# Conv attention on Trainium2: values as two float16 halves, a mix on four 32-column groups, sums from the exponential, and key copies on GpSimd

## The chip, the cores and the metric

The kernel runs on one core of one Trainium2 chip. The metric is the device time of one execution, in microseconds (us); the number quoted is the median of the runs. The engines are TensorE (PE; its weight loads are PEld), VectorE (DVE), ScalarE (ACT) and GpSimd (POOL); SyncE (SP) issues DMAs here.

## The reference

Two decoder layers run over x of 4 x 1024 x 256. The diff touches one of their six stages, the second layer's self attention, in which each head's scores pass a convolution of width 3 over the keys that mixes the 16 heads:

```python
Q = (query @ Wq.T + bq).reshape(b, s, h, dh).transpose(0, 2, 1, 3)      # h = 16, dh = 16
K, V = ...                                                             # likewise
scores = jnp.einsum('bhqd,bhkd->bhqk', Q, K) / np.sqrt(dh).astype(np.float32)
x = scores.transpose(0, 2, 1, 3).reshape(b * s, h, s)
x = lax.conv_general_dilated(x, conv_w, window_strides=(1,), padding=[(1, 1)], ...)
x = x + conv_b[None, :, None]
weights = jax.nn.softmax(x.reshape(b, s, h, s).transpose(0, 2, 1, 3), axis=-1)
out = jnp.einsum('bhqk,bhkd->bqhd', weights, V).reshape(b, s, e)
return out @ Wo.T + bo
```

## The kernel before

The stages run one behind the other. The conv attention (`stage_conv_attention`, L1858) moves the convolution to the keys: for each output head the three shifted keys of all heads are scaled with that head's taps and added, which gives one key matrix of 256 x 1024. So scores have a contraction of 256 instead of 16, and each is computed from high and low parts of queries and keys (QH, QL, KH, KL), three products for each of two blocks of 128 channels.

**Units.** A unit is 128 query rows of one head against 1024 keys. Eight units are a head, four are a group, 16 heads are a batch, 4 batches make 512 units. Every engine has its own hand-written loop over the units (`for u in range(ALL + TAIL)`), and semaphores tie the loops together. What is done for one unit `u`:

- TensorE, `scores(u)` (L2061): twelve matmuls of 512 columns into one of three PSUM buffers of 1024 columns. It waits until the low half of unit u - 3 is made, and at a head's first unit until both low key parts are there (`key_low`).
- VectorE, `maximum(u)` (L2320, L2324): negative maximum over the keys, then the bias for the exponential. After it `low_probs(u - 1)` (L2329).
- ScalarE, `exps(u)` (L2210): exponential in place in PSUM; `high_probs(u)` (L2217): its high half as float16 into `halves`. VectorE's `low_probs(u)` is the low half. Both are turned by a transposing DMA that SyncE issues (L1994) into `probsT`, one of three buffers of two units each.

**Groups.** Once in four units, after the scores of units 3 and 7 of a head, TensorE runs the mix (`mix_values`, L2075) of the four units that were turned last: for each of two pairs of units, 8 key tiles and 2 halves, so 32 matmuls of 256 columns. The stationary operand is `V`: 64 columns, of which 48 hold the values in three bfloat16 parts of 16, one holds ones (its product is the sum of the probabilities) and the rest zeros. The two halves write to PSUM partitions 0 to 63 and 64 to 127. ScalarE moves the result to SBUF (`move_mixT`, L2226), TensorE turns it back after units 1 and 5 (`turn_back`, L2085), and VectorE normalizes after units 2 and 6: L2339 adds the two sums, L2341 the six parts, L2345 inverts, L2348 multiplies.

**Keys of the next head.** While head hh is scored, GpSimd and ScalarE make the keys of hh + 1. For each of the two channel blocks GpSimd scales the middle tap (L2012) and adds the other two (L2016, L2020), which ScalarE has scaled (`tap`, L2200). ScalarE makes these in units 0 (block 0, third tap), 1 (block 1, first tap), 3 (block 1, third tap) and 6 (block 0 of the head after, first tap), each between the exponential and the high half. ScalarE then copies the high parts (`high`, L2206, in units 2 and 5), and GpSimd subtracts them for the low ones (L2027), both after all its additions.

**Values** are split by ScalarE (L2262) and VectorE (L2375, L2380) in turn, in four steps for each half of the heads, in units 101 to 104 of a batch for the next one and 5 to 8 for its second half.

**Extra work.** Between the units the next batch is prepared: normalization at units 36 to 48 of a batch, queries at 52 to 64, keys at 68 to 80, values at 84 to 96, one step in each group, after the scores of units 0 and 4 of a head; the last batch's output is turned and projected at units 3 to 16. All share one PSUM bank with `turn_back`.

## Time and profile before

| | us |
|---|---|
| median of 3 runs | 4005.49 (4002.89 to 4012.54) |
| span of the profiled execution | 4015.4 |
| conv attention in it: first score matmul to last turning of a mix | 867.0 to 2738.2 |
| score matmuls of 512 columns | 6144 in three groups, 681.7 + 637.7 + 637.3 busy |
| mix matmuls of 256 columns | 4096, 249.1 busy |

The profile is of one execution, so its span is set beside the median and not taken for it. Busy time of TensorE counts matmuls that overlap, and its ends are modelled; where a sentence needs TensorE's pace, the starts of its weight loads are read.

### The profile page before, as it was taken

The numbers are of one execution on the slowest core, as the hardware profiler recorded it, in microseconds if no ns is written. First come the engines' busy times: TensorE is split into PE (matmuls) and PEld (weight loads), VectorE is DVE, ScalarE is ACT, GpSimd is POOL, SyncE is SP. The second block draws the span as 40 slices with busy tenths as digits, with TensorE's granted clock in tenths as the row PEclk, the third lists the DMA queues.
The fourth block names the chain that finished last, engine by engine and source line by source line (L and its number), as shares of the span: only waits on it lengthen the run. The fifth ranks groups of instructions, "written<-read, shape, count | busy, mean of one in ns | idle before, by whom it ended". The sixth has DMA issues, their size and how long they took to land. (4 is left out here: it accounts for less than half of the span.)

```text
span 4015.4 us, 64275 instructions
## 1 busy us (share of the span) xinstructions
PE 3489.2 (87%) x22159; PEld 2787.0 (69%) x22159; DVE 2936.8 (73%) x5979; ACT 2563.5 (64%) x3388; POOL 1828.4 (46%) x1128
## 2 busy tenths in 40 slices
PE   6867623379999999999999999996889898799999
PEld 4645421257777777877777788884667667689999
DVE  4568789878878888788878888884767666464347
ACT  2334445558778887788878888882667666344433
POOL 0034410026655565565655656651767676360005
PEclk9988956599999999999999999997999999799999
DMA  1047700058878887787878878882559477643224
GB/s 49 0 95 128 147 5 1 1 142 150 143 139 148 140 147 140 139 153 136 151 137 141 153 140 155 153 157 56 99 91 171 84 124 137 199 138 97 76 78 144
DMA packets 1571361, 470.22 MB, mean 117 GB/s; under 512 B 1507175, under 2 KB 1565160, under 8 KB 1569768
## 3 DMA queue, kind: packets, MB, share of 16 engines
q1 hardware_dynamic: 1564903, 449.40, 58.8%
q0 software_dynamic: 6144, 16.79, 1.3%
q8 instruction: 179, 2.93, 0.3%
q14 instruction: 135, 1.10, 0.1%
HBM read 49.00 MB, written 39.58 MB: 22 GB/s over the span
## 5 line engine op out<-in xcount | busy, mean ns | idle before, releaser
L2320 DVE TENSOR_REDUCE d_neg_max<-psum 128x1 f32<-128x1024 f32 x512 | 624.9, 1220 | 247.9 <-PE psum L2061 242.3
L2210 ACT ACTIVATE psum<-psum,d_bias 128x1024 f32<-128x1024 f32 x512 | 557.6, 1089 | 335.3 <-DVE d_bias L2324 331.8
L2061 PE MATMUL psum<-d_KH,d_QH 128*128 128x512 f32 x2048 | 681.7, 414 | 17.7 <-DVE d_halves L2329 13.2
L2329 DVE SCALAR_TENSOR_TENSOR d_halves<-psum,d_halves 128x1024 f16<-128x1024 f32 x512 | 622.9, 1217 | 24.0 <-ACT d_halves L2217 21.2
L2061 PE MATMUL psum<-d_KL,d_QH 128*128 128x512 f32 x2048 | 637.7, 393 | 0.0
L2061 PE MATMUL psum<-d_KH,d_QL 128*128 128x512 f32 x2048 | 637.3, 392 | 0.0
L2020 POOL TENSOR_TENSOR d_KC<-d_KC,d_tap_of 128x1024 f32<-128x1024 f32 x126 | 301.8, 2395 | 559.9 <-ACT d_tap_of L2200 559.9
L2217 ACT ACTIVATE d_halves<-psum 128x1024 f16<-128x1024 f32 x512 | 521.7, 1019 | 3.5
L2061 PEld LDWEIGHTS psum<-d_KH,d_QH 128*128 128x128 f32 x2048 | 360.5, 189 | 129.4 <-issue 43.4
L2061 PEld LDWEIGHTS psum<-d_KH,d_QL 128*128 128x128 f32 x2048 | 385.1, 188 | 86.6
L2061 PEld LDWEIGHTS psum<-d_KL,d_QH 128*128 128x128 f32 x2048 | 384.8, 188 | 86.5
L2027 POOL TENSOR_TENSOR d_KL<-d_KC,d_KH 128x1024 fp32r<-128x1024 f32 x128 | 308.1, 2407 | 190.0 <-ACT d_KH L2206 190.0
L2916 POOL TENSOR_TENSOR e_halves<-e_probs,e_halves 128x1102 f16<-128x1102 f32 x128 | 292.4, 2284 | 124.0 <-ACT e_halves L3017 123.0
L2016 POOL TENSOR_TENSOR d_KC<-d_KC,d_tap_of 128x1024 f32<-128x1024 f32 x126 | 308.0, 2444 | 28.4 <-ACT d_tap_of L2200 20.4
L2200 ACT ACTIVATE d_tap_of<-d_K,d_taps 128x1024 f32<-128x1024 f32 x252 | 289.0, 1147 | 0.0
L2075 PE MATMUL psum<-d_probsT,d_V 128*64 128x256 f16 x4096 | 249.1, 275 | 2.3 <-DMA d_probsT<-d_halves 2.3
L2075 PEld LDWEIGHTS psum<-d_probsT,d_V 128*64 128x64 bf16 x4096 | 214.0, 110 | 49.0 <-issue 46.1
L3010 ACT ACTIVATE e_probs<-psum,e_neg_max 128x1102 f32<-128x1102 f32 x128 | 150.3, 1174 | 91.4 <-DVE e_neg_max L3089 91.3
L3085 DVE TENSOR_REDUCE e_own_neg_max<-psum 128x1 f32<-128x1102 f32 x128 | 167.1, 1305 | 4.4
L3474 POOL DMA_INDIRECT f_tile<-f_expert_out,f_slots x64 | 60.8, 951 | 236.3 <-DMA f_expert_out<-f_tile 183.8
L3761 DVE TENSOR_TENSOR f_hT_low<-psum,f_hT_high 128x384 fp32r<-128x384 f32 x135 | 75.2, 557 | 122.9 <-ACT f_hT_high L3637 110.7
L3017 ACT ACTIVATE e_halves<-e_probs 128x1102 f16<-128x1102 f32 x128 | 143.7, 1122 | 27.8 <-DMA e_probsT<-e_halves 24.6
(515 smaller groups left out, 7481.8 us busy)
## 6 DMA issues: line engine op xcount, KB each, us to landing
f_weights_raw<-in_L_ffn_packed_dram SPq DMA_DIRECT2D x10, 1088.0 KB, 16.0
f_tile<-expert_rows SPq DMA_DIRECT2D x71, 128.0 KB, 2.2
f_expert_out<-f_tile SPq DMA_DIRECT2D x71, 128.0 KB, 1.7
d_probsT<-d_halves SPq DMA_TRANSPOSE x512, 4.3
f_tile<-f_kept_rows SPq DMA_DIRECT2D x64, 128.0 KB
expert_rows<-d_group_mixT SPq DMA_DIRECT2D x7, 1024.0 KB, 11.6
residual_stream<-in_x_dram SPq DMA_DIRECT2D x4, 1024.0 KB, 9.5
f_kept_rows<-residual_stream SPq DMA_DIRECT2D x4, 1024.0 KB, 8.5
```

Of the source, the lines that this page charges most:

```text
L2016: g.tensor_tensor(KC[:, ch, :], KC[:, ch, :], tap_of[:, ch, :], ALU.add)\
L2020: g.tensor_tensor(KC[:, ch, :], KC[:, ch, :], tap_of[:, ch, :], ALU.add)\
L2027: g.tensor_tensor(KL[hh % 2][:, ch, :], KC[:, ch, :], KH[hh % 2][:, ch, :].bitcast(F32), ALU.subtract).then_inc(key_low.sem, 1)
L2061: last = t.matmul(scores_at(u)[:, cols], q_part[:, ch, j * P:(j + 1) * P], k_part[hh % 2][:, ch, cols], start=k == 0, stop=k == 5)
L2075: last = t.matmul(mix_bank[part * WIDE:(part + 1) * WIDE, at:at + 2 * P], V[:, k, h, :], probsT[p % 3][:, part * TB + k, :, :].rearrange(" ...
L2200: a.activation(tap_of[:, ch, :], K[b % 2][:, ch, k:S + k], ACT.Copy, scale=taps[:, ch, 3 * h + k:3 * h + k + 1]).then_inc(tapped.sem, 1)
L2210: a.activation(scores_at(u), scores_at(u), ACT.Exp, bias=bias[u % 2][:, 0:1])\
L2217: a.activation(halves[u % 4][:, 0, :], scores_at(u), ACT.Copy, scale=LIFT)\
L2320: v.tensor_reduce(neg_max[u % 2][:], scores_at(u), AXIS.X, ALU.max, negate=True)\
L2329: v.scalar_tensor_tensor(halves[u % 4][:, 1, :], scores_at(u), LIFT, halves[u % 4][:, 0, :], ALU.mult, ALU.subtract).then_inc(probs_low.se ...
L2916: g.tensor_tensor(halves[i % 3][:, 1, 0:W], probs[i % 3][:], halves[i % 3][:, 0, 0:W], ALU.subtract)\
L3085: v.tensor_reduce(own_neg_max[g % 2][:], scores_at(u), AXIS.X, ALU.max, negate=True)\
```

## The change

- **Values as two float16 halves.** `V` becomes 2 x 8 x 8 x 32 float16 columns a partition: 16 with the high half of the scaled values, 16 with the rest. ScalarE makes the high half (`values_high`), VectorE the low one (`values_low`). The scale is a power of two from a bound on the values: ScalarE squares and sums Wv and bv, TensorE adds over partitions, VectorE and GpSimd (a power of -1/2) make the scale, and ScalarE scales Wo once by its inverse, in unit 4.
- **Mix on four column groups.** 16 matmuls of 512 columns; four in a row write to PSUM partitions 0, 32, 64 and 96 on: two halves of the probabilities times two key tiles. `probsT` is now two buffers of four units.
- **Sums from the exponential** (`accum_out`), which puts an instruction that reads the accumulator behind it. The column of ones, L2339 and the memsets of `V` go. The reduction of the parts has 8 terms instead of 6.
- **Key high parts by GpSimd**, as `tensor_scalar` with two factors of 1.0, one before each low part; ScalarE's `high` goes.

```diff
-        V = sb("V", [P, TB, H, WIDE], BF16)
+        V = sb("V", [P, 2, TB, H // 2, 2 * HD], F16)
...
-        probsT = [sb(f"probsT{i}", [P, 2 * TB, 2, P], F16) for i in range(3)]
+        probsT = [sb(f"probsT{i}", [P, 2 * TB, 4, P], F16) for i in range(2)]
...
                 for u in range(ALL):
-                    p, i = u // 2, u % 2
-                    if i == 0 and p >= 3:
-                        sp.wait_ge(mixed.sem, mixed.at(p - 2))
+                    group, i = u // 4, u % 4
+                    if i == 0 and group >= 2:
+                        sp.wait_ge(mixed.sem, mixed.at(group - 1))
...
+                def high(hh, ch):
+                    g.wait_ge(scored.sem, scored.at(TB * (hh - 1)))
+                    g.wait_ge(tap_three.sem, tap_three.at(DC * hh + ch + 1))
+                    g.tensor_scalar(KH[hh % 2][:, ch, :], KC[:, ch, :], 1.0, 1.0, ALU.mult, ALU.mult)\
+                        .then_inc(key_high.sem, 1)
+
                 def low(hh):
                     for ch in range(DC):
+                        high(hh, ch)
                         g.wait_ge(scored.sem, scored.at(TB * (hh - 1)))
...
+                g.wait_ge(v_scaled.sem, v_scaled.at(2))
+                g.tensor_tensor(v_size[:, 1:2], v_size[:, 0:1], core.minus_half[:, 0:1], ALU.pow)\
+                    .then_inc(v_scaled.sem, 1)
...
-                    for k in range(TB):
-                        for part in range(2):
-                            last = t.matmul(mix_bank[part * WIDE:(part + 1) * WIDE, at:at + 2 * P], V[:, k, h, :],
-                                            probsT[p % 3][:, part * TB + k, :, :].rearrange("p i q -> p (i q)"),
-                                            start=k == 0, stop=k == TB - 1)
+                    for u in range(4 * group, 4 * group + 4):
+                        t.wait_ge(turned[u % 4].sem, unit_turned(u))
+                    t.wait_ge(mixT_moved.sem, mixT_moved.at(group))
+                    for k in range(0, TB, 2):
+                        for lane in range(4):
+                            part, tile = lane % 2, k + lane // 2
+                            last = t.matmul(mix_bank[lane * 32:(lane + 1) * 32, :], V[:, side, tile, h, :],
+                                            probsT[group % 2][:, part * TB + tile, :, :]
+                                            .rearrange("p i q -> p (i q)"), start=k == 0, stop=k == TB - 2)
...
-                def high(hh, ch):
-                    a.wait_ge(scored.sem, scored.at(TB * (hh - 1)))
-                    a.wait_ge(tap_three.sem, tap_three.at(DC * hh + ch + 1))
-                    a.activation(KH[hh % 2][:, ch, :], KC[:, ch, :], ACT.Copy).then_inc(key_high.sem, 1)
-
                 def exps(u):
                     a.wait_ge(bias_ready.sem, bias_ready.at(u + 1))
-                    a.activation(scores_at(u), scores_at(u), ACT.Exp, bias=bias[u % 2][:, 0:1])\
-                        .then_inc(probs_ready.sem, 1)
+                    a.wait_ge(inverted.sem, inverted.at(u // 4 - 3))
+                    a.activation(scores_at(u), scores_at(u), ACT.Exp, bias=bias[u % 2][:, 0:1],
+                                 accum_out=sums[u // 4 % 4][:, u % 4, :]).then_inc(probs_ready.sem, 1)
...
-                    v.tensor_reduce(prob_sum[:].rearrange("p u a -> p (u a)"), units[:, :, :, PARTS * HD], AXIS.X,
-                                    ALU.add).then_inc(sums_ready.sem, 1)
-                    v.tensor_reduce(group_sum[:], units[:, :, :, 0:PARTS * HD]
-                                    .rearrange("p u f (r e) -> p u e f r", r=PARTS), AXIS.XY, ALU.add)\
-                        .then_inc(parts_added.sem, 1)
-                    v.wait_ge(sums_ready.sem, sums_ready.at(group + 1))
-                    v.reciprocal(inv_sum[:], prob_sum[:]).then_inc(inverted.sem, 1)
+                    v.tensor_reduce(group_sum[:], parts, AXIS.X, ALU.add).then_inc(parts_added.sem, 1)
+                    v.wait_ge(probs_ready.sem, probs_ready.at(4 * group + 4))
+                    v.reciprocal(inv_sum[:], sums[group % 4][:]).then_inc(inverted.sem, 1)
...
+                def values_low(b, side):
+                    v.wait_ge(v_high.sem, v_high.at(2 * b + side + 1))
+                    v.scalar_tensor_tensor(value_half(side, 1), value_whole(side), v_scale[:, 0:1],
+                                           value_half(side, 0), ALU.mult, ALU.subtract).then_inc(v_low.sem, 1)
```

How the instructions stand on three engines in the middle of the first batch. GpSimd, one head's keys, before:

```order
L2012 TENSOR_SCALAR d_KC<-d_K,d_taps 128x1024
L2016 TENSOR_TENSOR d_KC<-d_KC,d_tap_of 128x1024
L2020 TENSOR_TENSOR d_KC<-d_KC,d_tap_of 128x1024
L2012 TENSOR_SCALAR d_KC<-d_K,d_taps 128x1024
L2016 TENSOR_TENSOR d_KC<-d_KC,d_tap_of 128x1024
L2020 TENSOR_TENSOR d_KC<-d_KC,d_tap_of 128x1024
L2027 TENSOR_TENSOR d_KL<-d_KC,d_KH 128x1024 x2
```

and after:

```order
L2014 TENSOR_SCALAR d_KC<-d_K,d_taps 128x1024
L2018 TENSOR_TENSOR d_KC<-d_KC,d_tap_of 128x1024
L2022 TENSOR_TENSOR d_KC<-d_KC,d_tap_of 128x1024
L2014 TENSOR_SCALAR d_KC<-d_K,d_taps 128x1024
L2018 TENSOR_TENSOR d_KC<-d_KC,d_tap_of 128x1024
L2022 TENSOR_TENSOR d_KC<-d_KC,d_tap_of 128x1024
L2028 TENSOR_SCALAR d_KH<-d_KC 128x1024
L2036 TENSOR_TENSOR d_KL<-d_KC,d_KH 128x1024
L2028 TENSOR_SCALAR d_KH<-d_KC 128x1024
L2036 TENSOR_TENSOR d_KL<-d_KC,d_KH 128x1024
```

ScalarE in units 0 to 3 of a head, before (L2210 exponential, L2217 high half, L2200 tap, L2206 key copy, L2226 move of a mix):

```order
L2226 ACTIVATE d_group_mixT<-psum 128x512
L2210 ACTIVATE psum<-psum,d_bias 128x1024
L2200 ACTIVATE d_tap_of<-d_K,d_taps 128x1024
L2217 ACTIVATE d_halves<-psum 128x1024
L2210 ACTIVATE psum<-psum,d_bias 128x1024
L2200 ACTIVATE d_tap_of<-d_K,d_taps 128x1024
L2217 ACTIVATE d_halves<-psum 128x1024
L2210 ACTIVATE psum<-psum,d_bias 128x1024
L2206 ACTIVATE d_KH<-d_KC 128x1024
L2217 ACTIVATE d_halves<-psum 128x1024
L2210 ACTIVATE psum<-psum,d_bias 128x1024
L2200 ACTIVATE d_tap_of<-d_K,d_taps 128x1024
```

and after, where each L2224 has the accumulator's read with it:

```order
L2240 ACTIVATE d_group_mixT<-psum 128x512
L2224 ACTIVATE psum,d_sums<-psum,d_bias 128x1024
L2218 ACTIVATE d_tap_of<-d_K,d_taps 128x1024
L2231 ACTIVATE d_halves<-psum 128x1024
L2224 ACTIVATE psum,d_sums<-psum,d_bias 128x1024
L2218 ACTIVATE d_tap_of<-d_K,d_taps 128x1024
L2231 ACTIVATE d_halves<-psum 128x1024
L2224 ACTIVATE psum,d_sums<-psum,d_bias 128x1024
L2231 ACTIVATE d_halves<-psum 128x1024
L2224 ACTIVATE psum,d_sums<-psum,d_bias 128x1024
L2218 ACTIVATE d_tap_of<-d_K,d_taps 128x1024
```

TensorE around a mix, before:

```order
L2061 MATMUL psum<-d_KL,d_QH 128x512 x2
L2061 MATMUL psum<-d_KH,d_QL 128x512 x2
L2075 MATMUL psum<-d_probsT,d_V 64x256 x32
L2061 MATMUL psum<-d_KH,d_QH 128x512 x2
L2061 MATMUL psum<-d_KL,d_QH 128x512 x2
```

and after:

```order
L2073 MATMUL psum<-d_KL,d_QH 128x512 x2
L2073 MATMUL psum<-d_KH,d_QL 128x512 x2
L2089 MATMUL psum<-d_probsT,d_V 32x512 x16
L2073 MATMUL psum<-d_KH,d_QH 128x512 x2
L2073 MATMUL psum<-d_KL,d_QH 128x512 x2
```

On GpSimd two copies come in behind the last addition, each ahead of a low part; on ScalarE the copy of unit 2 is gone (and that of unit 5, not shown), and the taps stand where they stood; on TensorE the mix stands where it stood, with half as many matmuls twice as wide.

## Rows read from the trace of the kernel before

**Rows 1.** The page: each engine's busy time, share of the span, instructions.
```profile
PE 3489.2 (87%) x22159; PEld 2787.0 (69%) x22159; DVE 2936.8 (73%) x5979; ACT 2563.5 (64%) x3388; POOL 1828.4 (46%) x1128
```

**Rows 2.** Busy time by stretch: three filled heads, three plain heads.
```profile
core 0: us, PE busy (x) PEld busy (x) DVE busy (x) ACT busy (x) POOL busy (x), PEclk, DMA share, GB/s
2075.00:2167.00 92.00, 92.00 (x543) 73.17 (x542) 71.71 (x103) 71.89 (x75) 49.97 (x25) 1.00 0.77 139
2398.00:2480.00 82.00, 81.89 (x505) 65.70 (x504) 70.40 (x97) 69.69 (x72) 52.18 (x27) 1.00 0.86 155
```

**Rows 3.** Waits, 900 to 2700 us: waiting instruction, releaser, total us, times, longest.
```profile
PEld psum L2061 <- DVE d_halves L2329: 26.5, 48, 1.9
```

**Rows 4.** Timeline of TensorE's weight loads in a plain head: start us, us, idle before.
```profile
2452.31 0.30 PEld L2061 LDWEIGHTS psum<-d_KH,d_QH 128*128 128x128 f32 x2 [0.20 <-issue]
...
2461.32 0.30 PEld L2061 LDWEIGHTS psum<-d_KH,d_QH 128*128 128x128 f32 x2 [0.47 <-DVE d_halves L2329]
...
2464.27 1.67 PEld L2075 LDWEIGHTS psum<-d_probsT,d_V 128*64 128x64 bf16 x32 [0.36 <-issue]
2466.14 0.30 PEld L2061 LDWEIGHTS psum<-d_KH,d_QH 128*128 128x128 f32 x2 [0.20 <-issue]
...
2479.67 0.30 PEld L2061 LDWEIGHTS psum<-d_KH,d_QH 128*128 128x128 f32 x2 [0.20 <-issue]
```

**Rows 5.** Timeline of a filled head: score loads at both ends, GpSimd's last addition.
```profile
2074.65 0.30 PEld L2061 LDWEIGHTS psum<-d_KH,d_QH 128*128 128x128 f32 x2 [0.20 <-issue]
...
2105.18 0.30 PEld L2061 LDWEIGHTS psum<-d_KH,d_QH 128*128 128x128 f32 x2 [0.20 <-issue]
...
2092.82 2.36 POOL L2020 TENSOR_TENSOR d_KC<-d_KC,d_tap_of 128x1024 f32<-128x1024 f32 x1 [4.35 <-ACT d_tap_of L2200]
```

**Rows 6.** Timeline of ScalarE in the latent attention stage: read and next instruction.
```profile
2904.20 0.19 ACT L3010 ACTIVATION_READ_ACCUMULATOR e_probs<-psum,e_neg_max 128x1 f32 x1
2904.43 1.12 ACT L3017 ACTIVATE e_halves<-e_probs 128x1102 f16<-128x1102 f32 x1
```

**Rows 7.** The plain head of rows 4, ScalarE.
```profile
2456.94 1.09 ACT L2210 ACTIVATE psum<-psum,d_bias 128x1024 f32<-128x1024 f32 x1 [0.72 <-DVE d_bias L2324]
2457.95 1.14 ACT L2200 ACTIVATE d_tap_of<-d_K,d_taps 128x1024 f32<-128x1024 f32 x1
...
2459.89 1.09 ACT L2210 ACTIVATE psum<-psum,d_bias 128x1024 f32<-128x1024 f32 x1
...
2463.90 1.05 ACT L2206 ACTIVATE d_KH<-d_KC 128x1024 fp32r<-128x1024 f32 x1
...
2467.78 1.14 ACT L2200 ACTIVATE d_tap_of<-d_K,d_taps 128x1024 f32<-128x1024 f32 x1
```

**Rows 8.** The same head, VectorE, from the low half of unit 1 on.
```profile
2462.99 1.22 DVE L2329 SCALAR_TENSOR_TENSOR d_halves<-psum,d_halves 128x1024 f16<-128x1024 f32 x1
2464.14 0.15 DVE L2339 TENSOR_REDUCE d_prob_sum<-psum 128x4 f32<-128x8 f32 x1
2464.21 0.55 DVE L2341 TENSOR_REDUCE d_group_sum<-psum 128x64 f32<-128x384 f32 x1
...
2465.22 1.21 DVE L2320 TENSOR_REDUCE d_neg_max<-psum 128x1 f32<-128x1024 f32 x1
```

**Rows 9.** The same head, GpSimd, the second half.
```profile
2469.07 2.41 POOL L2020 TENSOR_TENSOR d_KC<-d_KC,d_tap_of 128x1024 f32<-128x1024 f32 x1 [3.86 <-ACT d_tap_of L2200]
2471.43 2.40 POOL L2027 TENSOR_TENSOR d_KL<-d_KC,d_KH 128x1024 fp32r<-128x1024 f32 x1
2475.73 2.41 POOL L2027 TENSOR_TENSOR d_KL<-d_KC,d_KH 128x1024 fp32r<-128x1024 f32 x1 [1.90 <-ACT d_KH L2206]
```

**Rows 10.** Line L2012 over the stage: duration ns min/median/max.
```profile
L2012 POOL TENSOR_SCALAR d_KC<-d_K,d_taps x126: 1114/1125/2106, 861.5 to 2680.4; 128x1024 f32<-128x1024 f32 x126
```

**Rows 11.** Timeline where the stage starts: a power, the first score matmuls.
```profile
834.95 1.69 POOL L191 TENSOR_TENSOR d_ln_rstd<-d_ln_tmp,minus_half 128x8 f32<-128x8 f32 x1
...
867.02 0.73 PE L2061 MATMUL psum<-d_KH,d_QH 128*128 128x512 f32 x2 [3.68 <-DVE d_ln_xT L2368]
```

More of the change, by code:

```diff
@@ L1881, in stage_conv_attention @@
     v_ready = c("v_ready")
-    v_split = [c(f"v_part{i}") for i in range(PARTS)]
-    v_left = c("v_left")
+    v_high, v_low = c("v_high"), c("v_low")
+    v_bound = c("v_bound_steps")
+    v_scaled = c("v_scale_steps")
+    wo_scaled = c("wo_scaled")
     biased = c("biased")
@@ L1897, in stage_conv_attention @@
     probs_low = c("probs_low")
-    turned = [c(f"turned{i}") for i in range(3)]
+    turned = [c(f"turned{i}") for i in range(4)]
     mixed = c("mixed")
@@ L2143, in _ @@
                     columns(0, k, wq, bank(4 + k), q_summed)
+                t.wait_ge(v_bound.sem, v_bound.at(2))
+                t.wait_ge(k_ready.sem, k_ready.at(1))
+                t.matmul(PS[:, 0:1], core.ones[:], v_squares[:, 0:1], start=True, stop=True).then_inc(v_bound.sem, 1)
+                t.wait_ge(v_scaled.sem, v_scaled.at(1))
                 t.wait_ge(k_ready.sem, k_ready.at(4))
@@ L2220, in move_mixT @@
                 def move_mixT(group):
-                    a.wait_ge(mixed.sem, mixed.at(2 * group + 2))
+                    a.wait_ge(mixed.sem, mixed.at(group + 1))
                     if group:
@@ L2274, in _ @@
                 tap(1, 0, 0)
-                values(0, 0, 0)
+                a.wait_ge(v_scaled.sem, v_scaled.at(5))
+                values_high(0, 0)
                 for u in range(ALL + TAIL):
@@ L2292, in _ @@
                         tap(hh + 1, 1, j - 1)
-                    if j in (2, 5) and hh + 1 < H * B:
-                        high(hh + 1, j // 3)
                     if j == 6 and hh + 2 < H * B:
@@ L2310, in _ @@
                 norm_vector(v, n, 0)
-                for tile in range(TB):
-                    v.memset(V[:, tile, :, PARTS * HD:PARTS * HD + 1], 1.0)
-                    last = v.memset(V[:, tile, :, PARTS * HD + 1:WIDE], 0.0)
-                last.then_inc(cleared.sem, 1)
                 v.wait_ge(loaded.sem, loaded.at(16 * LOADS))
@@ L2332, in normalize @@
                 def normalize(group):
-                    units = back_bank.rearrange("p (u f e) -> p u f e", u=4, f=2)
+                    parts = back_bank.rearrange("p (u s e) -> p u e s", u=4, e=HD)
                     tile0, h = group % 2 * 4, group // 2 % H
```

134 lines of the change are left out of this document (70 added, 64 removed).

## The prediction, written before the changed kernel ran

> **What bounds the kernel now.** The conv attention stage runs from about 867 to 2740 us, so it holds nearly half of the span, and the diff touches nothing else. Over the whole span TensorE is the busiest engine, 87% [rows 1]. I read the busy time by stretch first, then the waits, then the order of time engine by engine inside one head, because the stage repeats itself head by head. A unit is 128 query rows of one head, a head is 8 units, a group is 4 units and one mix, and there are 64 heads. In three heads that carry no extra work for the next batch TensorE is busy 81.89 of 82 us at the full clock, VectorE 70.4, ScalarE 69.7 and GpSimd 52.2 [rows 2]. So TensorE sets the pace. Its waits for a PSUM bank (VectorE's low halves, L2329) are 26.5 us over 1800 us [rows 3]. The reader is to see that TensorE has no spare time, but that two others have only 14% and 15%.
>
> I call a head without extra work plain. One begins at 2452.31 and the next at 2479.67, which is 27.36 us [rows 4]. In it stand 8 units of twelve score matmuls, two mixes, two turns and one wait of 0.47 us at 2461.32. The mix at 2464.27 keeps its weight loads going for 1.67 us, with 0.36 us before and 0.20 us behind it [rows 4]. In the heads that also project keys, queries and values for the next batch (filled ones) a head takes 30.53 us: 2074.65 to 2105.18 [rows 5]. Read in the same way, by the first score weight load of each head, the 63 head periods fall in three kinds: 19 plain ones at 27.34 to 27.42, 28 long ones, most of them filled in both groups (29.1 to 34.1, most 30.5), and 16 between (28.1 to 28.9).
>
> **The mix on four column groups.** Before, 32 matmuls of 256 columns, two at once; after, 16 of 512 columns, four at once. The columns that stream are as many, but each step now carries four. Today's 32 starts lie 1.67 / 31 = 0.054 us apart [rows 4]: two streams of 256 columns side by side at the granted 2.4 GHz [rows 2] would be 0.053, so two groups run beside each other without loss. No row shows four. Bounds: four run as well as two do, then the starts stay 0.054 us apart and 16 take 15 x 0.054 = 0.81 us, 0.86 us less, of which the last matmul gives back 0.11 us since it is 256 columns longer: 0.75 us a mix. Or only two run at once, then 16 x 512 columns take as long as 32 x 256, and the gain is nothing. I take 0.75, since the rate of two is perfect and the same mechanism is only repeated; the other end is a rival. The 0.36 and 0.20 us around the mix stay, as the switch between widths stays. So a head loses 1.5 us of TensorE time: 25.86 us plain, 29.03 us filled.
> The Trainium skill speaks for less ("TensorE: Matmul & The Clock Gate", measured speedup vs the span model): three column groups of 32 with 512 columns gave 2.38 times. At that efficiency (79%) an estimate of the mix is 1.07 us, the gain 0.5 us instead of 0.75, and the sum below 15 us later, near 3965, inside the forecast's own range; no run here shows four groups.
>
> **Sums from the exponential.** The exponential gets a second instruction that reads the accumulator. In the later stage that does this it takes 0.19 us, and the next one starts 0.23 us behind it [rows 6]. Without it the step behind an exponential starts after 1.01 us (2456.94 to 2457.95 [rows 7]), so a unit with a tap between loses 0.20 us. 512 times 0.19 is 97 us on ScalarE, against 128 key copies of 1.05 us [rows 7] that leave it: ScalarE as a whole gets lighter. But the copies leave at units 2 and 5 of a head, and the reads come at all, those of units 0 and 1 too, which matter below.
>
> **VectorE.** The small sum (L2339) goes, the reduction grows from 384 to 512 elements a partition. 0.55 us for 384 and 1.21 us for 1024 [rows 8] give about 0.13 us for the 128 more; the small sum gave the next one its start after 0.07 us. I count 0.06 us more a group. The values lose one of three parts: one step of about 1.2 us less on VectorE and 1.05 on ScalarE, 8 times, beside other work.
>
> **Key copies on GpSimd.** This is what I think decides. GpSimd adds the taps of both channel blocks and then makes the low parts. Before, ScalarE made the high copies beside it; now GpSimd makes them itself, and the first one stands behind all tap additions, though its input is ready long before. Before, in a plain head the last addition starts at 2469.07, 16.76 us into the head, since it waits for the tap that ScalarE makes in unit 3 at 2467.78 [rows 7, 9]. The two low parts follow at 2471.43 and 2475.73, so keys are whole at 2478.14, 1.53 us before the next head begins [rows 4, 9]. After: addition 2.45, copy 1.21, low part 2.36, copy 1.21, low part 2.41, and 0.05 to TensorE: 9.69 us. The copy's 1.13 us is the median of 126 one-input instructions of the same size on the same engine [rows 10]; no row has it with the rounded output type, but the two-input one with that output takes 2.41 beside 2.41 without [rows 9], so the type is free. Bounds for one copy: 1.13 and, by the two-input row, 2.41; I take 1.13, since it reads one input.
> The start of the last addition moves too. Unit 3's tap follows unit 3's exponential, that the maximum at 2465.22, that the normalizing at 2464.14, and that the low half of unit 1 at 2462.99, which ScalarE sets: exponential 2456.94, tap, high half, exponential 2459.89, tap, high half [rows 7, 8]. There are no gaps in that chain, so both accumulator reads (0.40) and the longer reduction (0.06) lie on it. Keys are whole at 16.76 + 0.46 + 9.69 = 26.91 us in a plain head. TensorE would be done with the head at 25.86, or up to 26.6 when I follow the PSUM waits that the faster mix leaves (0.67 us at unit 3, 0.1 to 0.3 at three others). So it waits for keys, and **a plain head takes 26.9 us**, 0.45 less rather than 1.5. In a filled head the last addition starts at 2092.82, 18.17 us in [rows 5]; with 0.46 and 9.69 that is 28.3, below 29.03: TensorE still sets it, and the 1.5 us are won.
>
> **Stage start.** VectorE puts six one-column steps into the chain that ends with the values at 867.02, for which TensorE waited 3.68 us [rows 11]. A small step takes 0.15 us [rows 8], some 0.25 with the handoff to the next, so 1.5 us. GpSimd makes one power (1.69 us at 834.95 [rows 11]) and then the first head's copies and low parts, 1.21 + 2.36 + 1.21 + 2.41 = 7.2 us; from about 857.5, when VectorE has the power's input, that ends at 866.4, just before the values. VectorE's two-input steps there collide with it, for another 1 to 2 us. The memsets that go were hidden. I count 3 us lost, between 1 and 5. Scaling Wo once at unit 4 is some 0.6 us of ScalarE in a head with slack: nothing. The end of the stage has one short mix on the path: 1 us won.
>
> **The sum.** 28 long heads x 1.5 = 42, less 2 for three heads in which VectorE's two-input steps collide with a busier GpSimd. 16 plain ones x 0.45 = 7; in the other three plain ones the queries of the next batch make the last addition later and keys come at 27.4, as now: 0. The 16 between, each with its own start of the last addition: 3 x 0.8 + 3 x 1.2 + 9 x 0.5 + 0 = 10. Together 57, minus 3, plus 1: 55 us. The profiled execution's span is 4015.4 us and would be 3960; the median of the runs is 4005.5, so the median becomes **3950 us**. What a measurement can tell here is about 0.3%, 12 us.
>
> **Rivals.**
> *TensorE alone sets every head.* If the key chain had slack, 63 x 1.5 = 94 less 2: 3913 us. For it: GpSimd is busy only 64% [rows 2]. Against it: its slack lies before the last addition, not behind it, and the margin is 1.53 us now [rows 4, 9] while 2.4 us of copies come in. It needs the chain of ScalarE and VectorE before unit 3's tap to get faster, and nothing makes it so. Chance 0.13.
> *Four groups run no faster than two.* The change then doesn't give what it says. Keys at 26.9 hide behind 27.36; the reads cost up to 0.2 us in 19 plain heads, the start 3: 4 + 3 = 7, so 4012 us. For it: no row shows four streams at once. Against: the 0.054 us [rows 4]. Chance 0.16.
> *Slower: the GpSimd copy costs like a two-input one.* With 2.0 us a copy the chain is 1.74 us longer and binds in 60 of 63 heads: 32 us more than now, 4037; with 2.41 it is 80 more, 4085. It turns from gain to loss where a copy takes 1.75 us. For it: two-input operations take 2.41 [rows 9], and a conversion could be slow. Against: the one-input row of 1.13 [rows 10]. Chance 0.11.
>
> **How the numbers follow.** Forecast 0.60, with its own range of 3930 to 3975: shorter by 14 if the accumulator reads are hidden, longer by 15 if each mix gains a third less than 0.75, and by 13 if a copy takes 1.3. The range for 8 in 10 reaches from 3915, which cuts half of the first rival, to 4015, which takes in the second and leaves out the third. Faster by over 0.3%: 0.60 + 0.13 = 0.73, and 0.01 of the second. Within: 0.15. Slower: 0.11.
>
> **What would show it.** In the profile after, the mix is 16 matmuls whose weight loads take 0.8 us from first to last: 1.6 refutes the step. In plain heads the first score load of a head waits for GpSimd's low part (about 1 us of a 26.9 us head), and in filled ones (29.0 us) not. The copies show 1.13 us. The last addition starts 17.2 us into a plain head; if at 16.8, the reads are hidden. If plain heads come out at 25.9, the key chain was no bound and I am wrong in the main point.

## The result, and the profile after

| | before | after |
|---|---|---|
| median, us | 4009.01 of 4 runs (4002.89 to 4019.19) | 3939.66 of 4 runs (3930.59 to 3953.26) |
| ratio, 95% interval | | 0.9828 (0.9809 to 0.9846) |
| span of the profiled execution | 4015.4 | 3938.1 |
| conv attention, its first to its last instruction | 1928.8 | 1865.9 |
| first score load of the stage to that of its last head, 63 heads | 1831.4 | 1769.1 |

The kernel is 69 us faster by the medians; 55 were forecast. In the profiles the stage is 62.9 us shorter, of which the 63 heads are 62.3. The further 14 us between the two profiled spans are for the most part not the change's: the last stage of the program, whose code is the same, took 556.8 us before and 545.2 here, and 551 to 563 in the ten further profiles below.

The page's line of busy times, which answers to [rows 1]:

```profile
PE 3378.2 (86%) x20113; PEld 2611.4 (66%) x20113; DVE 2943.8 (75%) x5833; ACT 2493.2 (63%) x3769; POOL 1962.5 (50%) x1257
```

TensorE lost 111 us of busy time and 2046 matmuls. GpSimd gained 134 us, ScalarE lost 70 and VectorE gained 7. The span fell by 77 us, less than TensorE's busy time: it now waits somewhere. Busy time by stretch, three filled heads and then three plain ones, as in [rows 2]:

```profile
core 0: us, PE busy (x) PEld busy (x) DVE busy (x) ACT busy (x) POOL busy (x), PEclk, DMA share, GB/s
2002.00:2088.00 86.00, 86.00 (x437) 63.13 (x436) 70.79 (x94) 69.18 (x95) 57.02 (x31) 1.00 0.82 147
2341.20:2420.90 79.70, 77.20 (x409) 57.82 (x409) 71.08 (x92) 66.61 (x91) 58.35 (x33) 1.00 0.89 159
```

In filled heads TensorE is busy all the time, as before; in plain ones it is idle 2.5 of 79.7 us, where it was idle 0.11 of 82. The waits of the stage (waiting instruction, releaser, total us, times, longest) say for whom, beside [rows 3]:

```profile
PEld psum L2073 <- POOL d_KL L2036: 39.8, 38, 1.3
...
PEld psum L2073 <- DVE d_halves L2338: 34.6, 69, 2.2
```

The first row did not exist before. It is GpSimd's low key part. Some 0.42 us of each of the 38 waits is the gap that stands behind any mix (below), so the keys themselves cost 0.63 us a wait on average, and 0.8 in the plain head below.

### The profile page after: what moved, and what is told of

It reads as the page before. It is cut to its first block and busy times, and to the rows that moved or that the text cites. A ratio compares the mean times of both kernels' runs of the same rounds, so it can differ in the third digit from the quotient of the medians.

```text
span 3938.1 us, 61085 instructions
## 1 busy us (share of the span) xinstructions
PE 3378.2 (86%) x20113; PEld 2611.4 (66%) x20113; DVE 2943.8 (75%) x5833; ACT 2493.2 (63%) x3769; POOL 1962.5 (50%) x1257
## 5 line engine op out<-in xcount | busy, mean ns | idle before, releaser
L2224 ACT ACTIVATE psum<-psum,d_bias 128x1024 f32<-128x1024 f32 x512 | 558.2, 1090 | 337.4 <-DVE d_bias L2333 332.5
L3651 ACT ACTIVATE f_silu<-psum 128x352 f32<-128x352 f32 x135 | 62.9, 466 | 145.2 <-PE psum L3541 142.2
L2333 DVE TENSOR_SCALAR d_bias<-d_neg_max,d_conv_b 128x1 f32<-128x1 f32 x512 | 139.8, 273 | 18.7
```

Of the source, the lines that this page charges most:

```text
L2224: a.activation(scores_at(u), scores_at(u), ACT.Exp, bias=bias[u % 2][:, 0:1], accum_out=sums[u // 4 % 4][:, u % 4, :]).then_inc(probs_read ...
```

## One plain head, one filled head

TensorE's weight loads in the plain head that begins at 2394.33 (start us, us, idle before), to be laid beside [rows 4]:

```profile
2394.33 0.30 PEld L2073 LDWEIGHTS psum<-d_KH,d_QH 128*128 128x128 f32 x2 [1.22 <-POOL d_KL L2036]
...
2403.45 0.30 PEld L2073 LDWEIGHTS psum<-d_KH,d_QH 128*128 128x128 f32 x2 [0.56 <-DVE d_halves L2338]
...
2406.41 0.55 PEld L2089 LDWEIGHTS psum<-d_probsT,d_V 128*32 128x32 f16 x16 [0.36 <-issue]
2407.39 0.30 PEld L2073 LDWEIGHTS psum<-d_KH,d_QH 128*128 128x128 f32 x2 [0.42 <-issue]
...
2420.89 0.30 PEld L2073 LDWEIGHTS psum<-d_KH,d_QH 128*128 128x128 f32 x2 [1.22 <-POOL d_KL L2036]
```

The head takes 26.56 us (27.36 before). From the mix's first load to the next score load are 0.98 us, where they were 1.87: a mix gains 0.89 us. Its single matmuls, whose starts the trace keeps, start in fours: four within 10 ns, the next four 216 ns after the first, and so on to 667 ns. Before they started in pairs every 109 ns, to 1665 ns. The head boundary is late: 1.22 us for GpSimd, which is this row of its timeline:

```profile
2411.32 2.40 POOL L2022 TENSOR_TENSOR d_KC<-d_KC,d_tap_of 128x1024 f32<-128x1024 f32 x1 [3.98 <-ACT d_tap_of L2218]
2413.69 1.05 POOL L2028 TENSOR_SCALAR d_KH<-d_KC 128x1024 fp32r<-128x1024 f32 x1
2414.89 2.41 POOL L2036 TENSOR_TENSOR d_KL<-d_KC,d_KH 128x1024 fp32r<-128x1024 f32 x1
2417.27 1.05 POOL L2028 TENSOR_SCALAR d_KH<-d_KC 128x1024 fp32r<-128x1024 f32 x1
2418.46 2.38 POOL L2036 TENSOR_TENSOR d_KL<-d_KC,d_KH 128x1024 fp32r<-128x1024 f32 x1
```

It waits 3.98 us for ScalarE's tap, makes its last addition 17.0 us into the head, and then runs without a gap until 2420.84; the scores start 0.05 us later. The reader is to see that the copies' input of block 0 was long there, and that 2.4 us of copies stand on the path. ScalarE, two accumulator reads on the way to that tap (compare [rows 7]):

```profile
2398.98 1.09 ACT L2224 ACTIVATE psum<-psum,d_bias 128x1024 f32<-128x1024 f32 x1 [0.40 <-DVE d_bias L2333]
2399.99 0.19 ACT L2224 ACTIVATION_READ_ACCUMULATOR psum<-psum,d_bias 128x1 f32 x1
2400.08 1.14 ACT L2218 ACTIVATE d_tap_of<-d_K,d_taps 128x1024 f32<-128x1024 f32 x1
```

The tap starts 1.10 us behind the exponential, where it was 1.01: a read of 0.19 us costs the next instruction 0.09. There are three such reads on the way to GpSimd's last addition, for unit 3's own exponential has one too:

```profile
2408.93 1.09 ACT L2224 ACTIVATE psum<-psum,d_bias 128x1024 f32<-128x1024 f32 x1 [1.59 <-DVE d_bias L2333]
2409.95 0.19 ACT L2224 ACTIVATION_READ_ACCUMULATOR psum<-psum,d_bias 128x1 f32 x1
2410.04 1.14 ACT L2218 ACTIVATE d_tap_of<-d_K,d_taps 128x1024 f32<-128x1024 f32 x1
```

A filled head takes 28.73 us (30.53 before), and its first score load has only the gap behind the mix:

```profile
2028.64 0.30 PEld L2073 LDWEIGHTS psum<-d_KH,d_QH 128*128 128x128 f32 x2 [0.42 <-issue]
...
2057.37 0.30 PEld L2073 LDWEIGHTS psum<-d_KH,d_QH 128*128 128x128 f32 x2 [0.42 <-issue]
```
```profile
2054.18 2.41 POOL L2036 TENSOR_TENSOR d_KL<-d_KC,d_KH 128x1024 fp32r<-128x1024 f32 x1
```

The last low part ends at 2056.59, so the keys are whole 0.78 us before the next head. By the kinds of the prediction, from the first score load of each head:

| | heads | forecast gain, us | measured gain |
|---|---|---|---|
| long | 28 | 42 - 2 | 41.3 |
| plain | 16 + 3 | 7 + 0 | 12.7 - 0.4 |
| between | 16 | 10 | 8.7 |
| start and end of the stage | | -3 + 1 | +0.6 |

Three of the long heads (3, 19 and 35) gained 2.5 us, for a reason of the kernel before. There a VectorE step of normalization began beside a GpSimd low part and took 2.18 us, where it takes 0.41 alone, and TensorE waited 1.90 us for the low half behind it; head 3 of before:

```profile
972.71 2.38 POOL L2027 TENSOR_TENSOR d_KL<-d_KC,d_KH 128x1024 fp32r<-128x1024 f32 x1
973.08 2.18 DVE L2402 TENSOR_SCALAR d_ln_xn<-residual_stream,d_ln_mean_var,d_ln_rstd 128x256 f32<-128x256 f32 x1
```

## Experiments

Theory K (key chain): in plain heads the end is set by ScalarE's tap of unit 3, then five steps of GpSimd; in filled heads by TensorE. Rivals: the wait only coincides with another; the reads or collisions between GpSimd and VectorE set the pace. A collision is here a VectorE step that takes far longer than it does alone while GpSimd works. Heads are numbered from 0 to 63 through the four batches; a stage or head time is always of one profiled execution. Ratios are to the kernel before on the same chip.

### Copies back on ScalarE

```diff
-                    g.tensor_scalar(KH[hh % 2][:, ch, :], KC[:, ch, :], 1.0, 1.0, ALU.mult, ALU.mult)\
-                        .then_inc(key_high.sem, 1)
...
-                        high(hh, ch)
...
+                    a.activation(KH[hh % 2][:, ch, :], KC[:, ch, :], ACT.Copy).then_inc(key_high.sem, 1)
...
+                    if j in (2, 5) and hh + 1 < H * B:
+                        high(hh + 1, j // 3)
```

> The changed kernel with the key copies on ScalarE again, in units 2 and 5 as before the change. Key chain theory: plain heads no longer wait for GpSimd's low part and take about 26.1 us, set by the matmuls (25.6) and PSUM waits, filled ones stay at 28.7; the whole kernel is 10 to 15 us faster than the changed one. Rival (VectorE and the PSUM banks set plain heads, and the wait for keys only coincides): plain heads stay at 26.6 and the kernel is within 3 us.

Measured: 3946.61 us, ratio 0.9811 (0.9779 to 0.9842). The stage takes 1850.2 us, 15.7 less than after, and the 63 heads 1750.7, 18.4 less. Plain heads take 25.9 to 26.25 (26.0 on average), filled ones 28.73. The head boundary no longer waits for keys, and what is late next is VectorE's low half in unit 1:

```profile
2415.49 0.30 PEld L2066 LDWEIGHTS psum<-d_KH,d_QH 128*128 128x128 f32 x2 [0.42 <-issue]
2418.87 0.30 PEld L2066 LDWEIGHTS psum<-d_KH,d_QH 128*128 128x128 f32 x2 [0.78 <-DVE d_halves L2340]
```

So this one part of the change costs the stage 14 to 18 us (beside a second profile of the changed kernel, below, it is 13.9 for the stage and 16.6 for the heads). On the whole program the two intervals overlap.

### The copies alone, on the kernel before

```diff
+                    g.tensor_scalar(KH[hh % 2][:, ch, :], KC[:, ch, :], 1.0, 1.0, ALU.mult, ALU.mult)\
+                        .then_inc(key_high.sem, 1)
...
+                        high(hh, ch)
...
-                    a.activation(KH[hh % 2][:, ch, :], KC[:, ch, :], ACT.Copy).then_inc(key_high.sem, 1)
...
-                    if j in (2, 5) and hh + 1 < H * B:
-                        high(hh + 1, j // 3)
```

> The kernel before with the key copies on GpSimd, and nothing else of the change. Key chain theory: keys are whole at 16.8 + 9.6 = 26.4 us of a plain head of 27.36, so the time stays within 4 us of the kernel before; a head is no longer or shorter. Rival (the copies are what made the kernel faster, by giving ScalarE 134 us back): 15 us or more faster.

Measured: 4015.65 us, ratio 0.9981 (0.9968 to 0.9994); 63 heads 1831.0 against 1831.4, plain 27.36, filled 30.53. In plain heads nothing is won or lost: the keys had 1.03 us to spare behind the slower mix. ScalarE's busy time falls by 111 us and that brings nothing where it waits for VectorE anyway. The same total hides some heads that moved, among them heads 16, 32 and 48, which take 0.6 us more. By the medians the kernel is 7.6 us faster, more than the 4 us expected; that is not in this stage (it is 2.3 us longer in the profile), and where it comes from is open.

### Each copy twice

```diff
                     g.tensor_scalar(KH[hh % 2][:, ch, :], KC[:, ch, :], 1.0, 1.0, ALU.mult, ALU.mult)\
+                        .then_inc(copied.sem, 1)
+                    g.wait_ge(copied.sem, copied.at(DC * hh + ch + 1))
+                    g.tensor_scalar(KH[hh % 2][:, ch, :], KC[:, ch, :], 1.0, 1.0, ALU.mult, ALU.mult)\
                         .then_inc(key_high.sem, 1)
```

> The changed kernel with each key copy on GpSimd made twice, the second behind the first: two more steps of 1.05 us with a handoff of some 0.1 to 0.15 us each, so 2.3 us more behind the last addition. Key-chain theory: a plain head has 0.05 us of slack and takes 2.3 us more, 28.9; a filled one has 0.78 and takes 1.5 more, 30.2 to 30.3; 63 heads 110 to 125 us more than 1769. This is what a GpSimd copy of about 2.2 us would have cost, the slower rival of the prediction. Rival, the wait for the low part only coincides with another that is as late (ScalarE or VectorE): plain heads under 28 and the stage less than 60 us longer.

Measured in one execution: 4102.93 us against 4021.91 for the kernel before. Filled heads take 30.22, as expected. But twelve of the 16 plain heads take 30.1 to 30.4 us, not 28.9, and the 63 heads 148.8 us more than after, not 110 to 125. The boundary waits 3.45 us, 2.2 more than after, as expected; some 1.6 us more come behind it (TensorE's loads, then busy time and PEclk of two stretches):

```profile
2571.05 0.55 PEld L2093 LDWEIGHTS psum<-d_probsT,d_V 128*32 128x32 f16 x16 [0.36 <-issue]
2575.05 0.30 PEld L2077 LDWEIGHTS psum<-d_KH,d_QH 128*128 128x128 f32 x2 [3.45 <-POOL d_KL L2040]
2575.39 0.63 PEld L2077 LDWEIGHTS psum<-d_KL,d_QH 128*128 128x128 f32 x2
2576.12 0.76 PEld L2077 LDWEIGHTS psum<-d_KH,d_QL 128*128 128x128 f32 x2
```
```profile
2555.00:2571.00 16.00, 15.88 (x82) 11.87 (x80) 14.36 (x20) 13.26 (x20) 11.71 (x8) 1.00 0.95 165
2575.10:2580.00 4.90, 4.90 (x15) 3.87 (x16) 0.35 (x2) 1.68 (x4) 4.60 (x3) 0.65 0.57 107
```

After the wait a pair of loads takes 0.76 us instead of 0.42, and the granted clock is 0.65 of full in these 4.9 us: mostly the lower level, 1.2 GHz. The other four plain heads are the control. They wait as long (3.33 to 3.48 us), keep the full clock, and take 28.8 to 29.0 us, the 28.9 that were expected. This is the head of 28.78 us that begins at 2666.05:

```profile
2666.05 0.30 PEld L2077 LDWEIGHTS psum<-d_KH,d_QH 128*128 128x128 f32 x2 [3.48 <-POOL d_KL L2040]
2666.40 0.42 PEld L2077 LDWEIGHTS psum<-d_KL,d_QH 128*128 128x128 f32 x2
```
```profile
2666.10:2671.00 4.90, 4.90 (x22) 4.01 (x23) 1.89 (x4) 1.98 (x5) 3.40 (x2) 1.00 0.58 109
```

So the same wait comes with the fall or without it, and what lies between 28.8 and 30.35 us is the clock. Over all boundaries of this execution, 27 of the 32 waits of 2.81 to 4.45 us have a lower clock in the 5 us behind them, and none of the 25 waits of 1.65 to 2.30 us has (filled heads wait 1.9 us and then run at full pace). 27 falls of 1.6 us are an estimated 43 of the 148.8 us, and the rest lies near the 110 expected. The slower rival of the prediction was real in its mechanism and priced too low. A copy with its handoff takes 2.34 us here, which is one of 2.26 us in its terms. By its two prices (32 us slower than before at 2.0, 80 at 2.41) that is 62 us slower than the kernel before; it is 81, though the mix is faster than the prediction reckoned.

### Without the sums

```diff
-                    a.activation(scores_at(u), scores_at(u), ACT.Exp, bias=bias[u % 2][:, 0:1],
-                                 accum_out=sums[u // 4 % 4][:, u % 4, :]).then_inc(probs_ready.sem, 1)
+                    a.activation(scores_at(u), scores_at(u), ACT.Exp, bias=bias[u % 2][:, 0:1])\
+                        .then_inc(probs_ready.sem, 1)
```

> The changed kernel without the sums of the exponentials: no accumulator and no instruction that reads it; heads are divided by the constant 100 instead of by their sums, so the normalization is left out. It isolates what the reads cost in time. Key-chain theory with what the trace after shows (0.09 us more between an exponential and a tap, units 0 and 1): plain heads 26.56 - 0.2 = 26.4, filled ones stay at 28.73, stage 3 to 8 us shorter. Rival, the reads are the cost of the change on ScalarE: 512 x 0.19 = 97 us of busy time, and the stage gets shorter by over 20 us, filled heads too. Only this stage is compared, since the later stages see other numbers.

Measured in one execution: plain heads 26.35 (26.56 after), filled 28.73; 63 heads 10.9 us less; stage 1859.0, which is 6.9 less and within the 3 to 8 expected. Theory K holds: 102 us of reads on ScalarE cost 0.2 us in a head whose end hangs on its tap, and nothing in a filled one. The heads alone gain more than the 16 plain ones explain, since heads between lose some 0.3 us each to the reads too.

### GpSimd's order: early low parts

Two kernels move block 0's copy and low part ahead. The first puts them right behind block 0's own additions:

```diff
-                    if hh:
-                        add_taps(hh)
-                    low(hh)
+                    for ch in range(DC):
+                        if hh:
+                            add_taps(hh, ch)
+                        low(hh, ch)
```

> The changed kernel with GpSimd's order changed: the copy and the low part of channel block 0 stand right behind its own tap additions, in the time in which GpSimd waits for the tap of unit 3, instead of behind those of block 1. Key chain theory: keys are whole some 3.5 us earlier, no head waits for them, plain heads about 26.1 us, 10 to 20 us faster than the changed kernel. Rival as in the run with the copies on ScalarE: 26.6 stays.

Measured: 3965.13 us, ratio 0.9861 (0.983 to 0.9892); stage 1873.0, 7 us longer than after. A miss. Keys are whole 2.63 us early, and plain heads take 26.87 all the same. ScalarE shows why:

```profile
2415.24 1.15 ACT L2217 ACTIVATE d_tap_of<-d_K,d_taps 128x1024 f32<-128x1024 f32 x1 [0.86 <-POOL d_KC L2017]
```

Its tap of unit 3 needs the buffer that block 1's first addition empties, and that addition now starts 14.4 us into the head instead of 10.6. The tap stands between exponential and high half, so ScalarE waits with the high half and the move of a mix behind it. VectorE then waits 1.24 us for that half, and TensorE stands still ahead of turning the mix back (L2098, which waits for ScalarE's move) and for VectorE's low half:

```profile
2444.78 0.42 PEld L2098 LDWEIGHTS psum<-ident,d_group_mixT 128*128 128x128 f32 x4 [0.97 <-issue]
2445.49 0.30 PEld L2072 LDWEIGHTS psum<-d_KH,d_QH 128*128 128x128 f32 x2 [0.29 <-DVE d_halves L2337]
```

The second puts them where GpSimd waits, between block 1's first and second addition:

```diff
-                    if hh:
-                        add_taps(hh)
-                    low(hh)
+                    if hh:
+                        first_taps_of(hh, 0)
+                        last_tap_of(hh, 0)
+                        first_taps_of(hh, 1)
+                    low(hh, 0)
+                    if hh:
+                        last_tap_of(hh, 1)
+                    low(hh, 1)
```

> Everything of the changed kernel, but GpSimd makes block 0's key copy and low part between block 1's first and second addition, where it would otherwise wait for ScalarE's tap of unit 3 (in the changed kernel from about 13 to 17.0 us into a plain head). Block 1's first addition stays where it was, so the tap buffer comes free for ScalarE as early as now (in e3_early_low it came 3.6 us later and the tap 1.1 us later, and plain heads took 26.87). Key-chain theory: the last addition starts at 17.0 to 17.3 us into a plain head and only one copy and one low part follow, so keys are whole at about 23 us; plain heads go from 26.56 to 25.9 to 26.1 as in e2_copies_act, filled ones stay at 28.73, and the kernel is 12 to 20 us faster than the changed one. Rival, GpSimd's two-input work holds up VectorE's two-input steps wherever it is put, so that moving it from unit 7 to units 4 and 5 costs as much as it brings: plain heads 26.4 to 26.9, no faster than the changed kernel.

Measured: 3946.51 us, ratio 0.9794 (0.9761 to 0.9827); 63 heads 1759.6, 9.5 less than after, not 12 to 20. Plain heads take 25.75, better than expected, and have 2.58 us of key slack. But the rival has a part in it too: heads 17, 33, 49 and 19, 35 take 0.7 us more than after, heads 4, 20, 36 0.6, some filled ones 0.2, and one (head 13) takes 32.07 where in after it took 28.24. VectorE and GpSimd in that head:

```profile
1231.73 3.47 DVE L2386 SCALAR_TENSOR_TENSOR d_V<-d_ln_xT,d_v_scale,d_V 128x1024 f16<-128x1024 f32 x1
```
```profile
1231.72 2.40 POOL L2017 TENSOR_TENSOR d_KC<-d_KC,d_tap_of 128x1024 f32<-128x1024 f32 x1 [1.83 <-ACT d_tap_of L2224]
```

VectorE's step with two SBUF inputs takes 1.28 us alone (869.10 in after). Here it began 0.01 us behind a GpSimd addition of 2.40 us and took 3.47, 1.08 us more than what was left of the addition. TensorE then waited 3.85 us for the low half, until 1237.83, and the granted clock was 0.63 from 1236 to 1240 and 0.51 from 1240 to 1244. The Trainium skill ("SBUF — State Buffer", SBUF: two separate sides) says that a VectorE step with two SBUF inputs and a GpSimd step that reads SBUF share ports as an exclusive lock for the whole instruction. That one waits for the other agrees with the trace; 1.28 + 2.40 = 3.68 would be the time by it, and 3.47 is 0.2 less. The kernel with the copies back on ScalarE has one such head too (31.75 us), in which a VectorE step of normalization takes 2.64 us instead of 0.41. The changed kernel has milder ones: the same VectorE step as above took 2.17 us in heads 13 and 29, beside a GpSimd scaling of 1.13 us (these heads take 28.24 and 28.60), and 1.27 in head 13 of the repeat below (27.35).

The third keeps after's order in the heads that had lost:

```diff
+                    late = h in (5, 9, 10, 14) or (h in (2, 4) and b > 0)
+                    if hh and late:
+                        last_tap_of(hh, 1)
                     low(hh, 0)
-                    if hh:
+                    if hh and not late:
                         last_tap_of(hh, 1)
                     low(hh, 1)
```

> As e9b_low_in_gap, but for the keys made in heads 1 (from the second batch on), 3 (likewise), 4, 8, 9 and 13 of a batch GpSimd keeps the changed kernel's order. These are the heads in which e9b_low_in_gap was slower than the changed kernel (by 0.2 to 0.7 us each) or, in head 13, in which a two-input step of VectorE stood 3.47 us behind a GpSimd addition once. Key-chain theory with these collisions: plain heads stay at 25.75, the heads named go back to the changed kernel's values, and 63 heads take about 1769 - 20 = 1749 us, so that the kernel is about 20 us faster than the changed one on the same chip. Rival: a collision only moves to the next two-input step, and 63 heads stay near 1760, 10 us faster.

> The changed kernel itself, for a comparison with e10_by_head on one chip: ratio to the kernel before 0.983, 63 heads 1769 us, plain heads 26.56, filled ones 28.73. If the time of a stage that the change does not touch (the last one took 545.2 us in its first profile and 554 to 562 in all others) is near 560 here, 11 us of the first gain were variation between executions.

Measured: 3943.31 us, ratio 0.9811 (0.9797 to 0.9824), beside the changed kernel's 3954.50 and 0.9837 (0.9822 to 0.9853) on the same chip: 11 us by the medians. The 63 heads take 1758.8 against 1767.3. The total is the rival's, 9 to 10 us short of what was expected. Of the shortfall some 3.3 to 4.2 us are head 13 of the first batch, which takes 31.55 again with another 3.48 us in the same VectorE step, at 1227.24 now: its place against GpSimd's additions drifts with what runs ahead of it, and a choice by head number doesn't hold it. Another 4 us are a mistake of the kernel's rule: in the last batch five plain heads without extra work kept the slow order too and take 26.56 instead of 25.75. Heads 4, 8 and 17 did go back to the changed kernel's values, heads 19 and 35 only in part (26.9; 26.6 after). The changed kernel's own repeat gave plain 26.56, filled 28.73, and 556.2 us for the last stage: its first 545.2 was variation.

By the stage alone the best kernel of all is the one with the copies back on ScalarE (1850.2), then those with the moved low part (1857.2 and 1857.7), then the changed kernel (1865.9 and 1864.1). On the whole program the intervals of neighbours overlap, so the order among the first three is open.

### The order of the four groups

First, the two groups of the even key tiles ahead of those of the odd ones:

```diff
-                    for k in range(0, TB, 2):
-                        for lane in range(4):
+                    for pair, k in [(i, j) for i in range(2) for j in range(0, TB, 2)]:
+                        for lane in (2 * pair, 2 * pair + 1):
```

> The changed kernel with the 16 mix matmuls in another order: first the two column groups of the even key tiles, then the two of the odd ones, so that only two groups can run beside each other. Same matmuls, same result. If the gain of the filled heads comes from four groups at once, each mix takes 0.85 us longer and a filled head 30.4 to 30.5 us instead of 28.7; a plain head, which waits for keys, loses only what is over its wait: 27.3 to 27.5 instead of 26.6. In all some 70 us more than the changed kernel. If the order doesn't matter (the fewer instructions are what helps), filled heads stay at 28.7.

Measured: 3955.44 us, ratio 0.9838 (0.9811 to 0.9864); filled 28.77, plain 26.56, 63 heads 1767.7. A full miss: forcing two groups at a time in program order changed nothing. Either waiting matmuls are passed by others, or a group does two at a time. So the groups one by one:

```diff
-                    for k in range(0, TB, 2):
-                        for lane in range(4):
+                    for lane in range(4):
+                        for k in range(0, TB, 2):
```

> The changed kernel with the 16 matmuls of a mix in another order: all four of one 32-column group in a row, then the four of the next. Three readings of why the order in e1_two_lanes made no difference. First, matmuls of groups that are idle start ahead of one that waits for its group: the mix stays at 0.9 to 1.0 us, heads as in the changed kernel. Second, starts stay in order, but a group takes two matmuls at a time: the groups follow one another two by two, about 1.7 us a mix, filled heads 28.73 + 1.5 = 30.2. Third, starts strictly in order and one at a time in a group: 16 x 0.216 = 3.5 us a mix, filled heads about 33.7, 63 heads more than 250 us longer.

Measured in one execution: filled heads 28.81, plain 26.56, 63 heads 1769.5. Its mix:

```profile
2063.76 0.58 PEld L2089 LDWEIGHTS psum<-d_probsT,d_V 128*32 128x32 f16 x16 [0.36 <-issue]
2064.77 0.30 PEld L2073 LDWEIGHTS psum<-d_KH,d_QH 128*128 128x128 f32 x2 [0.42 <-issue]
```

1.01 us against 0.98. The single starts are 0, 13, 27, 40 ns, then 226, 239, 253, 266, and so on. In program order neighbours are issued about 3.3 ns apart, and 13 is four of them: these are the first matmuls of each group, and the second ones follow 216 ns behind. (With two groups at a time the first four are at 0, 3, 27, 30, that is instructions 0, 1, 8 and 9.) So each column group works off its own matmuls in order, and one that waits for its group doesn't hold up those of the other groups. The trace doesn't name the group of a single start; the reading rests on these distances and on the total. The Trainium skill ("TensorE: Matmul & The Clock Gate", What overlaps and what doesn't) calls matmuls strict FIFO, without reordering; by that the last of 16 would start after 12 waits of 0.216 us, and with the 0.31 us behind the last start of after's mix this is an estimate of 2.9 us; the run shows 1.01, so here it does not hold for starts.

## Why the prediction was right, point by point

- **The stage and the engine that sets it: right.** Filled heads at 28.73, forecast 29.03; plain ones wait for GpSimd's low part.
- **The mix: right mechanism, mis-sized.** 0.75 was forecast, 0.89 measured. The step that failed is "the starts stay 0.054 us apart and 16 take 15 x 0.054 = 0.81 us". Starts are not evenly spread: four start together, so the last is 3 x 0.216 us behind the first plus 0.01, 0.67 us, not 0.81. Before, too, they came in pairs, and 1.67 us was the last of 16 pairs. Counting rounds gives it: 16 x 0.109 = 1.74 before, 4 x 0.216 = 0.86 after, 0.88 less. The Trainium skill's speedup of 2.38 for three groups ("TensorE: Matmul & The Clock Gate", Measured speedup vs the span model) would by the prediction's estimate have given 0.5; these four groups did better.
- **Plain heads: right mechanism, too pessimistic.** 26.9 forecast, 26.56 measured. The last addition starts at 16.99 instead of 16.76 + 0.46 = 17.22. The two reads of units 0 and 1 bring the low half of unit 1 0.21 later, not 0.40, and from there to the maximum it is 0.07 less, not 0.06 more: in after the maximum starts 1.01 us behind the reduction, where it was 1.08 behind the small sum. Unit 3's own read, which the prediction left out, adds 0.09. Together 0.23, and the kernel without reads gains 0.21 a plain head. The part behind the addition was put at 9.69 and is 9.57, since a copy takes 1.05 and not 1.13. The prediction had named both sizes as what to look for: 17.2, or 16.8 if the reads are hidden. The truth is between. That TensorE by itself might need up to 26.6 was wrong: where keys are early, plain heads take 25.75 to 26.0.
- **Copies on GpSimd: right.** 1.05 us at the median of 128 and 1.24 at most, and the move costs the changed kernel 14 to 18 us of its stage, shown by taking it back. The prediction told where the cost comes from, but not that the change without this part is better.
- **Between and long heads: sum right, parts not.** Forecast 50, measured 50.0. The 15 heads filled in both groups gained 1.8 each instead of 1.5. Heads 3, 19 and 35 gained 2.5, by luck: the meeting of VectorE and GpSimd that held them before doesn't come about after. Against that, heads 16, 32 and 48 lost 0.6, heads 4, 20, 36 and 15, 31, 47 some 0.14 each, which was not foreseen. For heads 16, 32 and 48 the copies on GpSimd are the cause: alone on the kernel before they bring the same 0.6, and with them back on ScalarE these heads gain 0.2. The allowance of 2 us for collisions is about what heads 13 and 29 lost.
- **Start and end of the stage: wrong, and small.** 3 us of cost were forecast for the start and 1 us of gain for the end. From the stage's first instruction to its first score matmul are 36.49 us before and 36.07 after (36.27 in the repeat), so the start cost nothing; from the last head's first score load to the last instruction 60.87 and 60.74 (60.52), and 59.0 to 62.9 in the other profiles, so the last mix's gain doesn't show. The step that failed is the price of the chain at the start: GpSimd's power took 0.55 us for 128 x 1 where the row of 128 x 8 had 1.69, the small VectorE steps took 0.14 to 0.16 us with little between them, and TensorE's wait before the first score fell from 3.68 to 2.65.
- **The three rivals.** "TensorE alone sets every head" is refuted: 38 waits for low parts. "Four groups no faster than two" is refuted: 0.98 us. "The copy costs like a two-input one" is refuted at 1.05, and its price was tested in one execution: it would have been worse than told, through the clock.
- **The total: inside the range, a little low.** By the profiles the stage gives 63 of the 69 us; the repeat gives 65 us by the medians and 64.7 in the stage. The 8 us between the stage's gain and the forecast are the plain heads (5.3) and the start and end (2.6); that the long heads and those between came out at their sum of 50 is partly luck, since a faster mix (4 us), the vanished waits of heads 3, 19 and 35 (3 us) and the heads that lost cancel.

## What to carry to other kernels

When an engine on the critical path gets faster, find the next chain at each boundary and add up what the same change puts on it: here a helper engine's copies, harmless in filled heads, cost some 40% of the possible gain in plain ones (0.79 us won a head, 1.35 without them on it). Matmuls of small output packed on column groups should be counted in rounds of one matmul's length, not by the mean spacing of starts. A step may be moved only with its buffers: the same two GpSimd instructions cost 7 us one place earlier than where they brought 9, since another engine's tap buffer hung on what they were moved past.

## What the runs showed of the hardware that was not expected

- Four 32-column groups run without loss beside each other: 16 matmuls of 512 float16 columns in 0.98 us, rounds of 216 ns at the full clock, in whatever order they are issued (0.98, 1.00 and 1.01 us for three orders).
- The accumulator's read takes 0.19 to 0.24 us in the trace and costs the next, independent instruction of ScalarE 0.09 us (a tap) to 0.11 us (a high half).
- TensorE's granted clock stayed at full through waits of 1.2 to 2.3 us and fell to the lower level in 27 of 32 waits of 2.81 to 4.45 us in one execution; in five of them, 3.33 to 3.48 us long, it stayed at full. With the fall a wait of 3.45 us costs nearly half as much again behind it: 1.6 us in plain heads.
- A VectorE step with two SBUF inputs that starts beside a GpSimd step ends only after it (1.28 us alone, 2.17 beside a scaling of 1.13, 3.47 beside an addition of 2.40), and such a meeting can come or go when unrelated work ahead of it shifts by less than a microsecond.
